# An attention and feed-forward chain on one core: row sums of a head group turned once, inverted on VectorE and brought back as broadcast rows through DRAM

## The chip, the cores and the metric

One NeuronCore of one Trainium2 chip runs the whole program. The metric is the device time of one execution in microseconds (us), the median of several runs. Engines are named as in the profile: PE (TensorE's matmuls) and PEld (its weight loads), DVE (VectorE), ACT (ScalarE), POOL (GpSimd), SP (SyncE, which here issues nearly all DMAs, in the order of its queue).

## The reference, cut to what matters

Eight batches of 512 rows of 512 numbers pass through two transformer layers: a cross attention of 16 heads of 64, then a self attention of 16 heads of 32, a cross attention of 16 heads of 32 and a feed-forward part of width 2048, each with a residual and a layer norm.

```python
# layer 0: heads of 64, added scores and a key mask
attn = softmax(where(mask == 0, NEG_INF, (q @ w_q)h * scale @ (k @ w_k)h.T + add_attn))
out  = (attn @ (v @ w_v)h) @ w_o + residual ; layer norm
# layer 1: heads of 32
x = _ln(x + _mha(x, x, ..., mask)); x = _ln(x + _mha(x, memory, ..., None))
x = _ln(x + relu(x @ w1 + b1) @ w2 + b2)
# the softmax's division by the sum of its row is what the change is about
```

## The kernel before, in words

The program is written engine by engine, with semaphores. It has four attention stages, `L0a` and `L0b` (8 heads of 64 each: the two halves of layer 0), `SA` and `CA` (16 heads of 32), and then the feed-forward part. Every stage runs over the eight batches. Work of one batch is laid out in slots: slot s holds the score product (`SCORE`) of tile s, a tile being 128 query rows of one head against 512 keys. There are 4 tiles to a head, so 32 slots to a batch in `L0a` and `L0b` and 64 in `SA` and `CA`. A head group is what fills 128 columns of output: two heads (8 tiles) or four (16 tiles), so there are 4 groups to a batch and 128 in the run. The tables `WIDE` (L0a, L0b), `SECOND` (SA) and `THIRD` (CA) give, for each step, its slot after the last head's first tile of a group; every engine runs its share of the steps in the order of these slots, and `STEPS` breaks ties.

A tile's way: PE makes the scores in one of two PSUM banks `psS` (L1547, L1548 or L1551). DVE takes them out with the row's smallest value (`MAX`, L2084 or L2088) into one of the tiles `PR`. ACT makes the exponential in place and leaves the row's sum in a column of `SM` (`EXP`, L1883). Then either PE turns the tile with four 128x128 transposes into one of three PSUM banks `psT` (`TURN`, L1572) and DVE or ACT copies it out (`P_LO`, L2180; `P_HI`, L1902), or the tile is split into half words (`SPLIT`, L2188, L1892 or L2464) and turned by two DMAs through `split_rows` (`BOUNCE`, L1349; `FETCH`, L1357), both on SP's queue. The value product of a group (`PV`, L1603) goes to the one PSUM bank `psV`, with rows that are not yet divided by their sums.

The division, as it was: DVE inverts the group's sums `SM` (128x8 or 128x16 numbers) into `RS` (`RECIP`, L2109). POOL spreads them to 128x512 in `RB`, which is the fourth tile of `PR` (`SPREAD`, L2475). PE turns that with four transposes into a bank of `psT` (`R_TURN`, L1580). ACT copies `psV` to `OG`, once the last use of `OG` (`GROUP_LO`, L2120) is over (`GATHER`, L1867). DVE multiplies the two (`SCALE`, L2114). ACT and DVE then make the two parts of `OT`, the input of the output product (`GROUP_HI`, L1876; `GROUP_LO`, L2120). In `SA` and `CA` these two steps of a batch's first group stand late, at slots 22.5 to 25, since `OT` is still read by the output product of the batch before. Because `RB` is a tile of `PR`, the tiles rotate over three buffers and tiles 7 and 15 share the fourth with it.

The order in which an engine works is fixed, so an instruction that waits holds back everything behind it. The score product of a tile waits until the bank of the tile two before it has been taken out by DVE:

```python
pe.wait_ge(s_evac, tal["s"].done(n - 2))
```

## Time and profile before

| | |
|---|---|
| median of 3 runs | 3869.85 us (3869.42 to 3872.04) |
| span of the profiled execution | 3867.5 us |
| the runs' median over that span | 2.35 us more (launch and end) |
| PE busy | 3727.1 us, 96% |
| DVE, ACT, POOL busy | 70%, 58%, 50% |
| DMA: mean of the 16 engines | q1 52.8%, q10 3.3% |

The profiled execution's own time is its span, 3867.5 us, with 2.35 us around it to the median of the runs. A row of a timeline begins with the start of the instruction from the span's start and its length, both in us; xN at its end says that N like it follow each other. Idle time before an instruction stands in brackets, with what ended it. Matmuls are pipelined: the next one starts before the one before has ended, so what one costs is read from start to start.

### The profile page before, as it was taken

Reading aid. Unit: us, or ns where it says so; the run is one execution under the profiler, and the core shown is the slowest. Engines: PE = TensorE matmul, PEld = TensorE weight load, DVE = VectorE, ACT = ScalarE, POOL = GpSimd, SP = SyncE. Lnnn points to the kernel's source line nnn. Section 1 sums busy time; section 2 is a strip of 40 time slices with the busy share of each in tenths; the row PEclk is TensorE's granted clock in tenths of the full one; section 3 lists DMA queues with packets and bytes.
Section 4 is the critical chain, followed back from the end, with each engine's and each line's share of the span. In section 5 each row is a group of like instructions: output and inputs, shape, how many; then the busy total and the mean of one; then the engine's idle time right before and its main releaser. Section 6 shows DMA issues by size and latency. Waiting matters only on the chain.

```text
span 3867.5 us, 63405 instructions
## 1 busy us (share of the span) xinstructions
PE 3727.1 (96%) x20588; PEld 2777.3 (72%) x20588; DVE 2714.5 (70%) x5753; ACT 2233.2 (58%) x4852; POOL 1950.0 (50%) x1981
## 2 busy tenths in 40 slices
PE   9999999999999998999999999999999989999999
PEld 6767777677777766777676766666766768888887
DVE  6666666577777768888888887888888864444434
ACT  6555555555555546888888777788777762111111
POOL 5544445444544445777777656677676642111101
PEclk9999999999999999999999999999999999999999
DMA  6677777545544566666666547666666773122200
GB/s 191 196 207 208 198 193 203 143 136 140 136 132 133 136 185 172 172 172 169 170 169 169 149 145 191 175 169 161 168 169 166 180 218 98 61 71 68 67 26 33
DMA packets 867943, 584.64 MB, mean 151 GB/s; under 512 B 641824, under 2 KB 690976, under 8 KB 866592
## 3 DMA queue, kind: packets, MB, share of 16 engines
q1 hardware_dynamic: 853648, 538.63, 52.8%
q10 hardware_dynamic: 13968, 41.95, 3.3%
q8 instruction: 169, 2.77, 0.3%
q14 instruction: 158, 1.29, 0.1%
HBM read 189.29 MB, written 237.50 MB: 110 GB/s over the span
## 4 chain that ended last, share of the span: by engine, by line
PE 44%; POOL 5%; ACT 5%; issue 5%; DVE 5%; DMA 1%; SPq 0%; DVEq 0%; ACTq 0%; POOLq 0%
PE psV L1603 6%; PE psT L1572 5%; POOL QS L2440 4%; PE psS L1551 4%; PE psJ L1496 3%; PE psJ L1498 3%; PE psJ L1497 3%; PE psS L1498 3%; PE psS L1496 3%; PE psS L1497 3%; PE psT L1496 2%; PE psT L1498 2%; PE psT L1497 2%; ACT PR L1883 2%; PE psT L1580 1%
## 5 line engine op out<-in xcount | busy, mean ns | idle before, releaser
L2440 POOL TENSOR_SCALAR QS<-QK 32x1024 fp32r<-32x1024 f32 (+2 forms) x1152 | 1241.5, 1078 | 858.3 <-DVE QK L2102 435.5
L1883 ACT ACTIVATE PR<-PR,MN 128x512 f32<-128x512 f32 x1536 | 1100.9, 718 | 515.9 <-DVE MN L2084 419.7
L2084 DVE CUSTOM_DVE_ANT_0 PR<-psS,RAW 128x512 f32<-128x512 f32 x1024 | 694.4, 682 | 437.6 <-PE psS L1548 344.2
L1572 PE MATMUL psT<-ID,PR 128*128 128x128 f32 x3912 | 597.0, 275 | 59.4 <-ACT PR L1883 58.4
L1572 PEld LDWEIGHTS psT<-ID,PR 128*128 128x128 f32 x3912 | 470.2, 141 | 211.2 <-ACT PR L1883 110.4
L1603 PE MATMUL psV<-plain 128*32 128x512 f32 (+1 forms) x3072 | 509.0, 609 | 18.2 <-DMA plain<-split_rows 12.5
L1551 PE MATMUL psS<-QS 128*128 128x512 f32 x1024 | 450.6, 442 | 23.2 <-DVE PR L2088 9.2
L2088 DVE TENSOR_SCALAR_CACHE_REDUCE PR<-psS 128x512 f32<-128x512 f32 x512 | 345.4, 682 | 101.1 <-PE psS L1551 98.3
L1922 ACT ACTIVATE PR<-psS,COLS 128x512 f32<-128x512 f32 x128 | 88.3, 690 | 562.6 <-PE psS L1498 562.6
L2180 DVE COPY plain<-psT 128x512 f32<-128x512 f32 x530 | 361.6, 682 | 1.0 <-PE psT L1572 0.8
L1902 ACT ACTIVATE plain<-psT 128x512 f32<-128x512 f32 x448 | 263.9, 589 | 129.6 <-PE psT L1572 127.3
L2154 DVE CAST QK<-PR 128x512 fp32r<-128x512 f32 x128 | 62.3, 487 | 352.1 <-ACT PR L1922 317.2
L1883 ACT ACTIVATION_READ_ACCUMULATOR PR<-PR,MN 128x1 f32 x1536 | 290.7, 189 | 0.0
L1603 PEld LDWEIGHTS psV<-plain 128*32 128x32 f32 (+1 forms) x3072 | 113.9, 118 | 229.2 <-issue 206.7
L1551 PEld LDWEIGHTS psS<-QS 128*128 128x128 f32 x1024 | 194.4, 190 | 106.5 <-DVE PR L2088 31.3
L1496 PE MATMUL psJ<-xT,W 128*128 128x512 f32 x640 | 264.1, 413 | 3.4 <-POOL xT L2388 2.0
L2357 POOL TENSOR_TENSOR Y<-Y,ROWS 128x512 f32<-128x512 f32 x96 | 135.1, 1425 | 237.8 <-DMA Y<-x 226.9
L1498 PE MATMUL psJ<-xT,W 128*128 128x512 f32 x640 | 251.3, 393 | 0.0
L1497 PE MATMUL psJ<-xT,W 128*128 128x512 f32 x640 | 251.1, 392 | 0.0
L2102 DVE SCALAR_TENSOR_TENSOR QK<-psJ,COLS,QK 128x512 fp32r<-128x512 f32 x256 | 190.6, 745 | 80.6 <-ACT QK L1859 80.4
L1547 PE MATMUL psS<-QS 128*128 128x512 f32 x512 | 233.2, 455 | 10.7 <-DVE MN L2084 6.1
L1859 ACT ACTIVATE QK<-psJ,COLS 128x512 fp32r<-128x512 f32 x256 | 173.9, 679 | 112.2 <-PE psJ L1498 86.6
(162 smaller groups left out, 8433.2 us busy)
## 6 DMA issues: line engine op xcount, KB each, us to landing
split_rows<-plain SPq DMA_DIRECT2D x366, 256.0 KB, 2.6
split_rows<-RAW SPq DMA_DIRECT2D x192, 256.0 KB, 2.5
x<-Y SPq DMA_DIRECT2D x96, 256.0 KB, 2.4
RAW<-x SPq DMA_DIRECT2D x96, 256.0 KB, 3.4
Y<-x SPq DMA_DIRECT2D x96, 256.0 KB, 3.2
kept_c<-R SPq DMA_DIRECT2D x32, 512.0 KB, 4.4
kept<-ROWS SPq DMA_DIRECT2D x32, 512.0 KB, 3.8
R<-kept_c ACTq DMA_DIRECT2D x8, 2048.0 KB, 9.0
```

The costliest lines, as they stand in the source:

```text
L1496: nc.tensor.matmul(dst, a[0], b[0], start=first, stop=False)
L1497: nc.tensor.matmul(dst, a[0], b[1], start=False, stop=False)
L1498: return nc.tensor.matmul(dst, a[1], b[0], start=False, stop=last)
L1551: mm = nc.tensor.matmul(psS[:, n % 2], q[:, tile], kk, start=True, stop=True)
L1572: mm = nc.tensor.transpose(dst[:, kt * P:(kt + 1) * P], prob(st, k)[:, kt * P:(kt + 1) * P], ID[:, :])
L1603: mm = nc.tensor.matmul(psV[j * dk:(j + 1) * dk], value(st, h, kt), probs(ring(st, b, h), kt), start=kt == 0, stop=kt == NT - 1)
L1883: nc.scalar.activation(prob(st, k), prob(st, k), ACT.Exp, bias=MN[:, k % 8:k % 8 + 1], scale=-1.0, accum_out=row_sums(st, SM, g)[:, qt, j: ...
L1902: nc.scalar.activation(probs_of(ring(st, b, h), qt), full, ACT.Copy).then_inc(p_copied, 1)
L2084: nc.vector.tensor_tensor_reduce(out=prob(st, k), in0=psS[:, n % 2], in1=FB[:, k % NT], scale=-st.scale, scalar=BIG, op0=ALU.add, op1=ALU. ...
L2088: nc.vector.tensor_scalar(prob(st, k), psS[:, n % 2], -st.scale, None, ALU.mult, ALU.min, accum_out=MN[:, k % 8:k % 8 + 1]).then_inc(s_eva ...
L2180: nc.vector.tensor_copy(probs_of(ring(st, b, h), qt), full).then_inc(t_evac, 1)
L2440: nc.gpsimd.tensor_scalar(to, pair, 1.0, 1.0, ALU.mult, ALU.mult).then_inc(stacked, 1)
```

## The change

The sums of a group are no longer spread before they are turned. `SM` is now two tiles of 128x128, zero outside the sums; PE turns one of them with one transpose as soon as the group's last exponential is done. The first 8 or 16 rows of the result hold one row of 128 queries for each head and query tile. DVE inverts these rows straight out of PSUM into `RT` (8x128 or 16x128). SP stores `RT` to `r_rows` in DRAM (`R_STORE`) and loads each head's row of 512 numbers back as 64 or 32 equal rows of `OG` (`R_LOAD`: two loads a group in L0a and L0b, four in SA and CA). DVE multiplies `psV` by `OG` into `OG`. The steps `SPREAD`, `PASS` and `GATHER` are gone, `R_TURN` and `RECIP` stand earlier or later in the tables, and `PR` rotates over all its four buffers. The output that ACT's `SQUARE` writes only for its sum goes to free parts of other tiles in place of `SPARE`. The rest of the diff keeps the orders and waits right.

```diff
 WIDE = {
...
-    "GATHER": 10.75,
-    "RECIP": 8,
-    "SPREAD": 9.5,
-    "R_TURN": 10.5,
-    "PASS": 11,
-    "SCALE": 12,
+    "R_TURN": 5,
+    "RECIP": 5.5,
+    "R_STORE": 6.5,
+    "R_LOAD": 8,
+    "SCALE": 11.5,
...
 SECOND = {
...
-    "GATHER": 10.5,
-    "RECIP": 5,
-    "SPREAD": 6,
-    "R_TURN": 10.25,
-    "PASS": 11,
-    "SCALE": 12,
+    "R_TURN": 5.5,
+    "RECIP": 6,
+    "R_STORE": 6.5,
+    "R_LOAD": 9.5,
+    "SCALE": 11.5,
...
         PR = sb("PR", [P, 4, S])
-        RB = PR[:, 3]
...
-        SM = sb("SM", [P, 2, 4 * NT])
-        RS = sb("RS", [P, 2, 4 * NT])
+        SM = sb("SM", [P, 2, P])
+        RT = sb("RT", [P, P])
...
         def prob(st, k):
 
-            if k in beside(st):
-                return PR[:, 3]
-            return PR[:, (k - sum(1 for b in beside(st) if b < k)) % 3]
+            return PR[:, k % 4]
...
+            def r_store(tile):
+
+                n = group_at[tile]
+                sp.wait_ge(*evacuated[tile[0], tile[1], ("R", tile[2])])
+                if n > 2:
+                    sp.wait_ge(r_full, loaded_of[n - 2])
+                rows = stage_of[tile[0]].per_group * NT
+                sp.dma_start(r_rows[n % 2].rearrange("j (t q) -> (j t) q", t=NT)[0:rows], RT[0:rows, :]).then_inc(r_stored, 16)
+
+            def r_load(tile):
+
+                n, st = group_at[tile], stage_of[tile[0]]
+                sp.wait_ge(r_stored, 16 * n)
+                sp.wait_ge(o_lo, n)
+                for j in range(st.per_group):
+                    sp.dma_start(OG[j * st.dk:(j + 1) * st.dk, :], r_rows[n % 2, j:j + 1, :].to_broadcast([st.dk, S])).then_inc(r_full, 16)
...
             def turn_reciprocals(st, g, b):
-                i = tal["spread"].next()
-                pe.wait_ge(r_spread, tal["spread"].done(i))
+                pe.wait_ge(exp_done, exp_at[st.name, b, st.per_group * NT * (g + 1) - 1])
                 dst = turn_place(st, b, ("R", g))
-                for tt in range(NT):
-                    mm = nc.tensor.transpose(dst[:, tt * P:(tt + 1) * P], RB[:, tt * P:(tt + 1) * P], ID[:, :])
-                mm.then_inc(t_full, 1)
+                nc.tensor.transpose(dst[:, 0:P], SM[:, g % 2], ID[:, :]).then_inc(t_full, 1)
...
-            def gather(st, g):
...
-                nc.scalar.activation(OG[:, :], psV[:, :], ACT.Copy).then_inc(pv_evac, 1)
...
-            def row_reciprocals(st, g):
-                i = tal["exp"].marked(NT * ((g + 1) * st.per_group - 1) + NT - 1)
-                dve.wait_ge(exp_done, tal["exp"].done(i))
-                nc.vector.reciprocal(row_sums(st, RS, g), row_sums(st, SM, g)).then_inc(recip_done, 1)
+            def row_reciprocals(st, g, b):
+                dve.wait_ge(t_full, turned_at[st.name, b, ("R", g)])
+                dve.wait_ge(r_stored, 16 * (group_at[st.name, b, g] - 1))
+                rows = st.per_group * NT
+                nc.vector.reciprocal(RT[0:rows, :], turned((st.name, b, ("R", g)))[0:rows, 0:P]).then_inc(t_evac, 1)
 
             def scale_group(st, g, b):
-                dve.wait_ge(t_full, turned_at[st.name, b, ("R", g)])
-                dve.wait_ge(pv_evac, tal["pv_own"].done(tal["pv_own"].n - 1))
-                nc.vector.tensor_tensor(OG[:, :], turned((st.name, b, ("R", g))), OG[:, :], ALU.mult).then_inc(t_evac, 1)
+                n = tal["pv"].next()
+                dve.wait_ge(r_full, parts_loaded[st.name, b, g])
+                dve.wait_ge(pv_full, tal["pv"].done(n))
+                nc.vector.tensor_tensor(OG[:, :], psV[:, :], OG[:, :], ALU.mult).then_inc(pv_evac, 1)
...
-            def spread(st, g):
```

How the steps stand now is shown at the second head group of batch 2 of `SA`, the one in which the rows of the timelines below lie. On DVE, around the reciprocal, before (the first row with 512 is `MAX`, `ISA MN` reads out its result, `COPY plain<-PR` is `SPLIT`, `COPY plain<-psT` is `P_LO`):

```order
L2109 RECIPROCAL RS<-SM 128x16 [waits exp_done]
L2084 ISA PR,MN<-psS,RAW 128x512 [waits s_full,t_full]
L2084 ISA MN 128x1
L2188 COPY plain<-PR 128x1024 [waits bounced0,exp_done]
L2084 ISA PR,MN<-psS,RAW 128x512 [waits s_full,t_full]
L2084 ISA MN 128x1
L2180 COPY plain<-psT 128x4x128 [waits t_full]
```

The same place now:

```order
L2088 ISA PR,MN<-psS,RAW 128x512 [waits s_full,t_full]
L2088 ISA MN 128x1
L2114 RECIPROCAL RT<-psT 16x128 [waits r_stored,t_full]
L2194 COPY plain<-PR 128x1024 [waits bounced0,exp_done]
L2088 ISA PR,MN<-psS,RAW 128x512 [waits s_full,t_full]
L2088 ISA MN 128x1
```

The reciprocal has moved one `MAX` later, stands right ahead of a `SPLIT`, and waits for PE's turn in place of ACT's exponential.

On PE, around that turn, now (`psS<-QS` is `SCORE`, `psJ<-W,OT` the output product of the batch before):

```order
L1585 MATMUL psT<-ID,PR 128x128 x4
L1509 MATMUL psJ<-W,OT 128x512
L1510 MATMUL psJ<-W,OT 128x512
L1511 MATMUL psJ<-W,OT 128x512
L1591 MATMUL psT<-ID,SM 128x128
L1564 MATMUL psS<-QS 128x512
L1509 MATMUL psJ<-W,OT 128x512
L1510 MATMUL psJ<-W,OT 128x512
```

It has taken its place ahead of a `SCORE`. Before, the four turns stood behind the value product of the group:

```order
L1572 MATMUL psT<-ID,PR 128x128 x4
L1551 MATMUL psS<-QS 128x512
L1603 MATMUL psV<-plain 32x512 x8
L1580 MATMUL psT<-ID,PR 128x128 x4
L1551 MATMUL psS<-QS 128x512
L1496 MATMUL psJ<-xT,W 128x512
```

The one turn of `SM` (`psT<-ID,SM`) stands about five slots earlier than the four turns of `RB` (the second `psT<-ID,PR`) stood, ahead of the value product.

On SP, between the loads of the sums and what follows them, now (`t_evac` is given by the reciprocal, `o_lo` by `GROUP_LO`, `r_stored` by the landing of the store):

```order
L1359 DMA r_rows<-RT 16x128 [waits r_full,t_evac]
L1341 DMA split_rows<-plain 128x1024 [waits fetched0,p_split]
L1254 DMA RAW<-x 128x512 [waits x_hi]
L1341 DMA split_rows<-plain 128x1024 [waits fetched1,p_split_act]
L1367 DMA OG<-r_rows 32x512 [waits o_lo,r_stored]
L1367 DMA OG<-r_rows 32x512 x3
L1349 DMA_TRANSPOSE plain<-split_rows 128x4x256 [waits pv_full,bounced0]
L1254 DMA RAW<-x 128x512 [waits x_hi]
L1300 DMA kept<-QS 128x2x512 [waits tile_lo]
```

One store and four loads have come in; the first load waits for the store and for the `GROUP_LO` of the group before, and the `FETCH` behind them waits with it.

## Rows read from the trace of the kernel before

**Rows 1.** The page, part 1: busy us (share of the span) xinstructions.
```profile
PE 3727.1 (96%) x20588; PEld 2777.3 (72%) x20588; DVE 2714.5 (70%) x5753; ACT 2233.2 (58%) x4852; POOL 1950.0 (50%) x1981
```

**Rows 2.** Windows L0a, L0b, SA, CA: us, busy of PE, PEld, DVE, ACT, POOL.
```profile
55.00:750.00 695.00, 676.87 (x3601) 492.83 (x3600) 433.37 (x911) 386.93 (x821) 337.95 (x321) 1.00 0.70 191
750.00:1460.00 710.00, 697.39 (x3691) 504.90 (x3690) 509.80 (x1055) 375.88 (x803) 312.64 (x341) 1.00 0.53 143
1460.00:2310.00 850.00, 806.55 (x5053) 590.06 (x5052) 731.40 (x1640) 661.74 (x1498) 585.92 (x582) 1.00 0.64 166
2310.00:3160.00 850.00, 798.83 (x4916) 574.39 (x4915) 710.99 (x1614) 660.06 (x1486) 562.18 (x563) 0.99 0.69 178
```

**Rows 3.** Groups by line: busy us, mean ns | idle before.
```profile
L2120 DVE SCALAR_TENSOR_TENSOR OT<-OG,COLS,OT 128x512 fp32r<-128x512 f32 x128 | 129.3, 1010 | 8.7 <-ACT OT L1876 7.6
...
L2475 POOL TENSOR_SCALAR PR<-RS 128x512 f32<-128x512 f32 x128 | 82.7, 646 | 146.2 <-DVE RS L2109 134.9 <-issue 9.5 <-POOL QS L2440 0.2
...
L1580 PE MATMUL psT<-ID,PR 128*128 128x128 f32 x512 | 81.9, 282 | 0.7 <-DVE plain L2180 0.7
L1867 ACT ACTIVATE OG<-psV 128x512 f32<-128x512 f32 x128 | 76.6, 599 | 180.3 <-PE psV L1603 175.0 <-DVE OT L2120 5.1
```

**Rows 4.** Timeline of PE, SA, batch 2, at two turns of four.
```profile
1709.51 0.60 PE L1572 MATMUL psT<-ID,PR 128*128 128x128 f32 x4
1709.86 0.48 PE L1496 MATMUL psJ<-W,OT 128*128 128x512 f32 x1
...
1724.18 0.66 PE L1580 MATMUL psT<-ID,PR 128*128 128x128 f32 x4
1724.59 0.47 PE L1551 MATMUL psS<-QS 128*128 128x512 f32 x1
```

**Rows 5.** Groups of DVE by line and shape: busy us, mean ns.
```profile
L2180 DVE COPY plain<-psT 128x512 f32<-128x512 f32 x530 | 361.6, 682 | 1.0 <-PE psT L1572 0.8
...
L2109 DVE RECIPROCAL RS<-SM 128x16 f32<-128x16 f32 x64 | 15.6, 243 | 0.5 <-ACT PR L1883 0.5
L2109 DVE RECIPROCAL RS<-SM 128x8 f32<-128x8 f32 x64 | 12.3, 192 | 0.0
```

**Rows 6.** Timeline of DVE, SA, batch 2, where the reciprocal will stand.
```profile
1715.98 0.68 DVE L2084 CUSTOM_DVE_ANT_0 PR<-psS,RAW 128x512 f32<-128x512 f32 x1
1716.59 1.06 DVE L2188 COPY plain<-PR 128x1024 uint16<-128x1024 uint16 x1
...
1717.57 0.67 DVE L2084 CUSTOM_DVE_ANT_0 PR<-psS,RAW 128x512 f32<-128x512 f32 x1
```

**Rows 7.** Timeline of PE, same place: three score products.
```profile
1716.78 0.40 PE L1551 MATMUL psS<-QS 128*128 128x512 f32 x1
...
1717.71 0.39 PE L1551 MATMUL psS<-QS 128*128 128x512 f32 x1
...
1718.39 0.47 PE L1551 MATMUL psS<-QS 128*128 128x512 f32 x1
```

**Rows 8.** Timeline of DVE, same group, around its GROUP_LO and SCALE.
```profile
1723.25 1.69 DVE L2120 SCALAR_TENSOR_TENSOR OT<-OG,COLS,OT 128x512 fp32r<-128x512 f32 x1
...
1726.68 0.68 DVE L2114 TENSOR_TENSOR OG<-psT,OG 128x512 f32<-128x512 f32 x1
```

**Rows 9.** Timeline of ACT, same stretch: the copy of psV.
```profile
1725.03 0.60 ACT L1867 ACTIVATE OG<-psV 128x512 f32<-128x512 f32 x1 [0.37 <-DVE OT L2120]
```

**Rows 10.** Timeline of SP, where the four row loads will stand.
```profile
1718.06 0.42 SPq L1263 DMA_DIRECT2D RAW<-x  x1
...
1721.21 1.28 SPq L1357 DMA_TRANSPOSE plain<-split_rows  x1
```

**Rows 11.** DMA issues: KB each, median us from issue to landing.
```profile
ROWS<-in_key_mask SPq DMA_DIRECT2D x15, 256.0 KB, 4.0
...
COLS<-in_cols SPq DMA_DIRECT2D x1, 20.0 KB, 2.6
```

**Rows 12.** Waits of PE over the run: us in total, times, longest.
```profile
PE psT L1572 <- ACT PR L1883: 58.4, 83, 1.8
```

More of the change, by code:

```diff
@@ L283 @@
     "PV": (8.5, 8.5, 9, 10),
-    "GATHER": 11,
-    "RECIP": 5,
-    "SPREAD": 6,
-    "R_TURN": 10,
-    "PASS": 11,
-    "SCALE": 12,
+    "R_TURN": 5.5,
+    "RECIP": 6,
+    "R_STORE": 6.5,
+    "R_LOAD": 9.5,
+    "SCALE": 11.5,
     "GROUP_HI": (22.5, 13.5, 12, 13.5),
@@ L413, in timetable @@
                 add(NT * h + table["PV"][kt], "PV", (g, kt))
-            add(NT * h + table["GATHER"], "GATHER", g)
-        if last:
-            for step in ("RECIP", "SPREAD", "R_TURN", "PASS", "SCALE", "GROUP_HI", "GROUP_LO"):
+            for step in ("R_TURN", "RECIP", "R_STORE", "R_LOAD", "SCALE", "GROUP_HI", "GROUP_LO"):
                 after = table[step]
@@ L871, in build @@
         QK = sb("QK", [P, 4, S], F32R)
+        with nc.sbuf_tensor("wide", [P, 2, 3, S], F32) as LOOSE:
+            pass
         QS = sb("QS", [P, 2, 3, S], F32R)
         PR = sb("PR", [P, 4, S])
-        RB = PR[:, 3]
         OT = sb("OT", [P, 2, NG, S], F32R)
@@ L1141, in build @@
         sent_at = {tile: n for n, tile in enumerate(orders["SPLIT"])}
+        loaded_of = {n: parts_loaded[tile] for tile, n in group_at.items()}
         split_at, splits = {}, {p_split: 0, p_split_act: 0, p_split_pool: 0}
@@ L1174, in tile_before @@
             last = STAGES[(i - 1) // B]
-            if k in beside(st):
-                return (st.name, b, ("R", 0)) if k == 15 else (last.name, (i - 1) % B, ("R", NG - 1)) if i else None
-            mine, others = ([n for n in range(s.steps) if n not in beside(s)] for s in (st, last))
-            at = mine.index(k) - 3
-            return (st.name, b, mine[at]) if at >= 0 else (last.name, (i - 1) % B, others[at + len(others)]) if i else None
+            return (st.name, b, k - 4) if k >= 4 else (last.name, (i - 1) % B, k - 4 + last.steps) if i else None
         order = weight_order()
@@ L1388, in run @@
                         {"F_LOAD": f_load, "F_BOUNCE": f_bounce, "F_FETCH": f_fetch}[step](at, k)
+                        continue
+                    if step in ("R_STORE", "R_LOAD"):
+                        b = batch + off if at is None else at
+                        (r_store if step == "R_STORE" else r_load)((st.name, b, k))
                         continue
@@ L1974, in run @@
                     elif step == "SQUARE":
-                        square(k)
+                        square(st, k, batch + off if at is None else at)
                     elif step == "CENTRE" and by_parts(st):
@@ L2014, in _ @@
             nc.vector.memset(COLS[:, NCOL:NCOL + NG], 0.0).then_inc(const_ready, 1)
+            nc.vector.memset(SM[:, :], 0.0).then_inc(const_ready, 1)
             dve.sem_inc(s_evac, 2)
@@ L2229, in run @@
                     elif step == "RECIP":
-                        row_reciprocals(st, k)
+                        row_reciprocals(st, k, batch + off if at is None else at)
                     elif step == "SCALE":
@@ L2507, in run @@
                         stack_piece(st, *k)
-                    elif step == "TURN" and k in beside(st):
-                        beside_turn[0] = turned_at[st.name, batch + off if at is None else at, k]
                     elif step == "SPLIT" and split_by_pool(st, k):
                         split_prob(st, k, batch + off if at is None else at)
-                    elif step == "SPREAD":
-                        spread(st, k)
                     elif step == "RES":
@@ L2517, in run @@
                         else:
-                            if st is None and k == 0:
-                                rows_of("FF")
+                            rows_of("FF" if st is None else st.rows)
                             residual(k)
```

89 lines of the change are left out of this document (38 added, 51 removed), and 4 rows, old and new, of the table SEAM.

## The prediction, made before the changed kernel ran

> **What bounds the kernel now.** I read the page's part 1 first: PE is busy 96% of the span, DVE 70% [rows 1]. Next come the windows of the four attention stages, since a mean over the run hides where another engine limits. In L0a and L0b PE is busy for 676.87 of 695 us and 697.39 of 710, while DVE has work for 62% and 72%. In SA and CA PE is busy for 806.55 and 798.83 of 850, and DVE for 86% and 84% [rows 2]. So the first two stages are PE's alone, and in the last two PE loses 43 and 51 us, with DVE close behind. The waits say how: the largest wait of PE is its turn waiting for an exponential, 58.4 us in 83 places [rows 12], and that exponential waits for DVE's `MAX`. The changed steps occur 128 times, 64 in L0a and L0b and 64 in SA and CA (16 batches of four groups). A thing saved on PE counts in full everywhere that PE is not waiting; a thing added on DVE is free in L0a and L0b, and in SA and CA it counts wherever `MAX` has no slack left.
>
> **PE: three turns fewer.** Four turns in a row last 0.60 us, and what follows starts 0.35 us after the first of them; since one lasts 0.27, their starts are (0.60 - 0.27) / 3 = 0.11 us apart [rows 3, 4]. The mean of 0.64 us busy a group [rows 3] is not what they cost, because they overlap their neighbours: from the first reciprocal turn to the next product it is 0.41 us [rows 4]. Three turns fewer are 0.33 us, times 128 = 42 us. The bounds are 0 (where PE waits for DVE anyway) and 0.41 us a group, 52 us, if the remaining turn hid altogether.
>
> **DVE: the reciprocal is the hidden price.** The scaling stays one 128x512 operation. The reciprocal goes from 8 or 16 numbers a partition to 128. It uses fewer partitions, but a partition's numbers pass one after another. An ordinary copy of 512 numbers lasts 682 ns, at most 1.3 ns a number; the reciprocal lasts 192 ns for 8 and 243 ns for 16 [rows 5], so (243 - 192) / 8 = 6.4 ns a number. For 128 numbers that is 243 + 112 x 6.4 = 0.96 us. The bounds are 682 / 4 = 0.17 us, if it ran like a copy, and 0.243 x 8 = 1.94 us, if the whole of it grew with the numbers. I take 0.96, because the two rows are the same operation. With the 0.2 us of the old one gone, DVE gains about 0.75 us of work a group, 96 us in all. 1.94 and 0.17 stay as the ends of the range.
>
> It also waits. It stands behind the `MAX` that ends at 1716.66, and PE comes to the turn only after the product that stands before the score at 1716.78 [rows 6, 7]. With 0.27 us for the turn, DVE can begin at about 1717.1, not at 1716.6: 0.5 us. So what stood at 1716.59, a `SPLIT`, begins 0.5 + 0.96 - 0.24 = 1.2 us later (0.24 is the old reciprocal, gone from just before), and so does the `MAX` behind it, at 1717.57, which ends at 1718.24. The next but one score, at 1718.39, needs the bank that this `MAX` frees [rows 6, 7]: 0.15 us of slack. PE loses 1.1 us. Behind it DVE has no pause up to the scaling, so the delay stays.
>
> In the three other groups of such a batch other work stands around the same slots. I take nothing for the first, whose reciprocal is soon followed by idle time, and 0.75 and 1.0 us for the third and fourth: a choice between nothing and the whole 1.2. A batch: 1.1 + 0.75 + 1.0 = 2.85 us, times 16 = 46 us. Bounds: 0, if the reciprocal costs 0.17 us and the turn is in time, and about twice that at 1.94 us. In L0a and L0b, where DVE is idle for 38% and 28% of the time [rows 2], I take 0.1 us a group, 6 us.
>
> **SP and the way through DRAM.** The copy of `psV` by ACT waited for the last use of `OG`: in the second group of a batch of SA or CA that is the `GROUP_LO` of the first group, which ends at 1724.94, and the copy starts 0.09 us later [rows 8, 9]. Now SP's loads wait for the same end. SP itself would be there at 1721.2 [rows 10], so `GROUP_LO` is what ends last. A DMA issue of a load takes SP 0.42 us [rows 10], so the last of four is issued 1.3 us after the first. The smallest DMA of the run, 20 KB, lands in 2.6 us, a 256 KB broadcast in 4.0 [rows 11]; one of these loads writes 64 KB. I take 1.3 + 2.5 = 3.8 us and the rows are there at 1728.7. DVE stands at `SCALE` at 1726.68 [rows 8]. It will wait 2.0 us, in the second group of each batch of SA and CA. Both ends of this comparison move together with DVE's delay, so that does not hide it. Bounds: 2.6 us in all (0.8 us of wait) and 1.3 + 4.0 = 5.3 (3.5 us of wait). Behind `SCALE` on DVE stand a `SPLIT` and two `MAX`, for which PE waits. 16 x 2.0 = 32 us. And in this group PE saves nothing, because DVE sets the pace: 16 x 0.33 = 5 us are given back.
>
> The Trainium skill gives a fixed cost of about 2.0 us for a DMA, most of it until the write is confirmed (DMA: Bandwidth & Descriptors, Anatomy of one DMA); it would leave the wait near 1.5 us, an estimate. No small load of rows is in this trace to decide.
>
> In the other groups `GROUP_LO` is long over, and the time for the loads is that from SP's place to `SCALE`, here 1726.68 - 1721.21 = 5.5 us [rows 8, 10]: above the 3.8, so I cost them at nothing. If the loads took 5.3 us they would begin to show, by perhaps 0.5 us in 48 groups, 24 us. In L0a and L0b the tables leave 3.5 slots of 710 / 256 = 2.8 us [rows 2], 9.7 us. The `FETCH` behind the loads comes up to 6 us later; the value product reads its tile some 15 slots on, at 850 / 512 = 1.7 us each, so nothing is late. The store goes out when the reciprocal ends, about 1718.1, and 2.6 us later it has landed, before `GROUP_LO` ends.
>
> **What else goes away.** POOL loses 128 spreads of 646 ns, ACT 128 copies of 599 ns [rows 3]. POOL is idle half of the time [rows 1]. ACT is busy 78% of SA and CA [rows 2], and the copy of `psV` itself came after idle time [rows 9]. Some of DVE's operations stretch (this `GROUP_LO` took 1.69 us, the mean is 1.01 [rows 3, 8]), perhaps beside POOL's, and fewer of these would help. I give 10 us for all this; between 0 and 30. The fourth buffer of `PR` lets `MAX` run one tile further ahead of the turns, but no wait of DVE for a turn is among the large ones: nothing. The memset of `SM` and the new waits at the start of the feed-forward part are under 1 us.
>
> **The sum.** -42 (turns) + 6 (reciprocals, L0a and L0b) + 46 (reciprocals, SA and CA) + 32 (waits for rows) + 5 (saving lost there) - 10 (POOL and ACT) = +37 us on the profiled 3867.5, and with the 2.35 us around it 3907 us. A local loss can shrink, since a late PE gives DVE room at the next place, so I go 2 us lower: 3905, 0.9% slower than the median of 3869.85.
>
> **Rivals.**
> 1. *PE's saving alone.* DVE's added work lies in its idle time (14 to 38% of the stages), and the rows are there when `SCALE` comes. For it: 96% on PE, and DVE never at 90%. Against it: 0.15 us of slack behind the second group's reciprocal, and a chain of 3.8 us for which there are 1.8. It gives 3870 - 42 = 3828, with the relief of ACT and POOL up to 10 less. It decides if the reciprocal lasts under 0.4 us, or if the rows land within 1.8 us of `GROUP_LO`. Chance 0.29.
> 2. *Half and half.* The reciprocal costs what I say, but its delay is mostly taken up by waits that PE has there already (43 and 51 us), and only the wait for the rows shows: -42 + 6 + 32 + 5 = about 3870, no change. Chance 0.17.
> 3. *A third price.* The broadcast loads land slowly, as the 4.0 us row says, and then the other groups of SA and CA wait too: 37 + 16 x 1.5 + 24 = 85 us, 3955. For it: all 32 rows of a load come from the same 2 KB. Chance 0.08.
> 4. *My forecast*, both DVE prices biting: 3880 to 3935. Chance 0.46.
>
> **How the numbers follow.** 0.2% of this time, 7.7 us, is about what a measurement of this kernel can tell from no change. Slower: 0.46 + 0.08 + 0.03 of the second case = 0.57. Same: 0.12 of the second case. Faster: 0.29 + 0.02 = 0.31. The range has to reach to the first rival, down to 3832 (some of that case lies below), and up to 3945. The forecast's own range is 3880 to 3935.
>
> **What would show it.** The reciprocal's row on DVE near 0.96 us, with idle time ended by PE's turn in SA and CA. `SCALE` idle before it about 2 us in one group of four of SA and CA, ended by a DMA, and no such wait in L0a and L0b. PE's idle time in the SA and CA windows up from 43 and 51 us to about 75 to 85 each, and the L0a and L0b windows shorter by some 8 us each. The prediction is wrong at its root if the reciprocal is short, or if the row loads land early.

## The result, and the profile after

The changed kernel takes 3944.89 us (median of 4 runs, 3942.07 to 3949.14) against 3870.94 for the kernel before on the same chip: 1.0187 times as long, interval 1.0173 to 1.0202 (the two medians alone would give 1.0191). That is 74 us more, where 35 had been forecast. The profiled execution has a span of 3940.3 us.

Part 1 of the page of the changed kernel answers to [rows 1], and the windows of its four attention stages and of the feed-forward part to [rows 2]. They are cut at most 2 us before each stage's first `MAX`, the last one at CA's last (each row: from and to, us, then the busy time of each engine with its instructions, the granted clock, the DMA share, GB/s):

```profile
PE 3715.4 (94%) x20204; PEld 2739.5 (70%) x20204; DVE 2763.4 (70%) x5754; ACT 2166.6 (55%) x4724; POOL 1895.6 (48%) x1853
```

```profile
25.00:734.00 709.00, 673.57 (x3542) 486.63 (x3541) 462.04 (x930) 381.79 (x812) 330.55 (x295) 1.00 0.72 203
734.00:1457.00 723.00, 689.67 (x3628) 498.91 (x3627) 527.00 (x1047) 356.88 (x765) 291.24 (x308) 1.00 0.57 151
1457.00:2326.00 869.00, 807.64 (x4928) 579.50 (x4926) 740.14 (x1652) 648.25 (x1472) 579.95 (x550) 0.99 0.67 175
2326.00:3212.00 886.00, 808.85 (x4842) 569.67 (x4843) 725.58 (x1626) 647.38 (x1466) 558.21 (x541) 0.99 0.70 177
3212.00:3940.00 728.00, 715.91 (x3169) 588.38 (x3167) 296.41 (x481) 120.91 (x193) 119.38 (x144) 0.99 0.24 69
```

Measured from `MAX` to `MAX`, the stages of the kernel before last 704, 710, 855, 853 and 720 us and those of the changed kernel 710, 724, 868, 887 and 727, so every one is longer now: by 6, 14, 13, 34 and 7. PE has fewer matmuls and does less in L0a and L0b, and still stands idle for 35 and 33 us there, where it was 19 and 11; in SA and CA it idles 61 and 77 us, where 75 to 85 each had been forecast.

The groups of DVE by line and shape (busy us, mean ns, then idle time before them and what ended it) answer to [rows 5]; the group of PE is that of the new turn:

```profile
L2120 DVE TENSOR_TENSOR OG<-psV,OG 128x512 f32<-128x512 f32 x128 | 87.8, 686 | 63.7 <-DMA OG<-r_rows 63.7
L2114 DVE RECIPROCAL RT<-psT 16x128 f32<-16x128 f32 x64 | 60.4, 944 | 29.0 <-PE psT L1591 29.0
L2114 DVE RECIPROCAL RT<-psT 8x128 f32<-8x128 f32 x64 | 60.2, 941 | 10.9 <-PE psT L1591 10.9
```

```profile
L1591 PE MATMUL psT<-ID,SM 128*128 128x128 f32 x128 | 36.9, 288 | 48.3 <-DVE plain L2186 46.4 <-ACT PR L1886 1.3
```

The reciprocal lasts about what was forecast, 0.94 us. `SCALE` waits for its rows, as forecast, but for more groups: of the 63.7 us, 29.4 are the second groups of SA and CA, 20.5 are CA's third groups and 13.1 are one single wait at CA's last group. And one wait was in no step of the prediction: PE's turn of the sums waits 46.4 us for DVE's `P_LO` (L2186), which takes an earlier tile out of `psT`; these are 48 waits of 1.0 us on average, 2.2 at most, and 43 of the 46.4 us lie in L0a and L0b. The timeline of PE in L0b shows one of the shorter ones, with the instruction behind it that starts as soon as the turn does, and the row of DVE that ends it (start, us, and in brackets the idle time before):

```profile
602.60 0.60 PE L1585 MATMUL psT<-ID,PR 128*128 128x128 f32 x4
603.47 0.30 PE L1591 MATMUL psT<-ID,SM 128*128 128x128 f32 x1 [0.27 <-DVE plain L2186]
603.52 0.48 PE L1509 MATMUL psJ<-xT,W 128*128 128x512 f32 x1
```

```profile
602.64 0.68 DVE L2186 COPY plain<-psT 128x512 f32<-128x512 f32 x1
```

The new turn comes directly behind that of a tile (602.60), and before that one PE had turned tiles at 601.70 and 598.72. There are three banks, so it needs the bank of the turn at 598.72, and DVE's copy frees a bank only at 603.32. The four old turns stood 5.5 slots later in the table.

In SA and CA the second group of a batch waits as forecast. This is DVE in CA, the place that answers to [rows 8]:

```profile
2729.38 1.24 DVE L2126 SCALAR_TENSOR_TENSOR OT<-OG,COLS,OT 128x512 fp32r<-128x512 f32 x1
...
2734.46 0.69 DVE L2120 TENSOR_TENSOR OG<-psV,OG 128x512 f32<-128x512 f32 x1 [2.02 <-DMA OG<-r_rows]
```

In CA the third group waits too, in seven of eight batches, and longer. Timelines of ACT, SP and DVE around one, and then the view of its row loads:

```profile
2860.44 0.33 ACTq L1793 DMA_DIRECT2D R<-kept_c  x1
```

```profile
2862.98 2.67 SPq L1367 DMA_DIRECT2D OG<-r_rows  x4
```

```profile
2872.08 0.69 DVE L2120 TENSOR_TENSOR OG<-psV,OG 128x512 f32<-128x512 f32 x1 [3.62 <-DMA OG<-r_rows]
```

```profile
L1367 SPq DMA_DIRECT2D OG<-r_rows x4: 434/532/1031, 2863.0 to 2865.2; - x4
...
DMA to landing us min/median/max: 5.4/6.5/7.2
```

The loads went out in time and took 6.5 us to land; 2.5 us ahead of them ACT had issued a load of 2 MB. The DMA issues of the run (KB each, median us to landing) have 2.1 us for such a load:

```profile
OG<-r_rows SPq DMA_DIRECT2D x128, 128.0 KB, 3.0
OG<-r_rows SPq DMA_DIRECT2D x256, 64.0 KB, 2.1
R<-kept_c ACTq DMA_DIRECT2D x8, 2048.0 KB, 9.5
```

Most of the 7 us behind CA is one wait of PE, before the value product of the last group; the profile does not say what ended it:

```profile
3227.87 5.90 PE L1613 MATMUL psV<-plain 128*32 128x512 f32 x32 [5.28 <-issue]
```

No wait of PE this long stands there in the other runs, whose feed-forward parts last 719 to 726 us. So of the 74 us some 5 may belong to this place alone.

### The profile page after: what moved, and what is told of

It reads as the page before. It is cut to its first block, busy times and chain, and to the rows that moved or that the text cites. A ratio compares the mean times of both kernels' runs of the same rounds, so it can differ in the third digit from the quotient of the medians.

```text
span 3940.3 us, 63021 instructions
## 1 busy us (share of the span) xinstructions
PE 3715.4 (94%) x20204; PEld 2739.5 (70%) x20204; DVE 2763.4 (70%) x5754; ACT 2166.6 (55%) x4724; POOL 1895.6 (48%) x1853
## 4 chain that ended last, share of the span: by engine, by line
PE 36%; DVE 7%; ACT 6%; issue 6%; DMA 4%; POOL 3%; SPq 1%; DVEq 0%; ACTq 0%; POOLq 0%
PE psV L1613 5%; PE psT L1585 4%; PE psS L1564 3%; PE psS L1509 3%; PE psS L1510 3%; PE psS L1511 3%; POOL QS L2444 3%; PE psJ L1509 2%; PE psJ L1510 2%; PE psJ L1511 2%; PE psT L1509 2%; PE psT L1511 2%; PE psT L1510 2%; ACT PR L1886 2%; DMA OG<-r_rows 2%
## 5 line engine op out<-in xcount | busy, mean ns | idle before, releaser
L2186 DVE COPY plain<-psT 128x512 f32<-128x512 f32 x530 | 360.3, 680 | 0.0
```

Source lines behind the costliest of these rows:

```text
L2186: nc.vector.tensor_copy(probs_of(ring(st, b, h), qt), full).then_inc(t_evac, 1)
```

## The experiments

Each run has its own kernel before beside it, so the times below are compared by their ratios to it; 0.1% is 3.9 us. Where a term is given in us it is the difference of two ratios times 3870, and uncertain by some 8 us. Intervals are about 0.15% either way. Lengths of stages come from each kernel's one profiled execution, between the first `MAX` of two stages, and for CA to the end of its last (704, 710, 855 and 853 us in the kernel before, 710, 724, 868 and 887 in the changed one). The diffs are shortened: entries of a table stand on one line, and helper lines are left out.

**turn_later: 1.0137 (1.0121 to 1.0152), 3921.31 us.**

```diff
-    "R_TURN": 5,   "RECIP": 5.5, "R_STORE": 6.5,
+    "R_TURN": 6,   "RECIP": 6.5, "R_STORE": 7,
```

> The changed kernel with three numbers of the table for L0a and L0b changed: R_TURN 5 becomes 6, RECIP 5.5 becomes 6.5, R_STORE 6.5 becomes 7. Theory A, that PE's turn of the sums stands too early and holds PE until a bank of psT is free (46.4 us of idle time before L1591, 43.3 of it in L0a and L0b): these waits fall under 10 us, PE idles 19 and 10 us again in the two stages, and the run is 25 to 40 us shorter than the changed kernel, 3905 to 3920. Theory B, that this wait only stands where PE would wait a moment later for DVE or ACT anyway: under 10 us shorter. If the rows then come late, DVE waits before SCALE in L0a and L0b, which it does not do now.

```profile
L1591 PE MATMUL psT<-ID,SM 128*128 128x128 f32 x128 | 35.9, 280 | 11.4 <-DVE plain L2186 10.8
```

The waits fell from 46.4 to 10.8 us, and the time by 0.50%, 19 us. L0b went back from 724 to 712 us. L0a did not get shorter (712 after 710): there PE's projections of the output now wait for DVE's sum, 9.0 us in 8 places, instead of 5.1 in 3, and 6.8 us of the stage run at a granted clock of 0.50, where the changed kernel had none. The rest of the profiled gain, 12 us, lies in SA, CA and the part behind, whose code is the same, so this pair alone leaves the price open between 9 and 19 us. A second pair helps: turn_rows is the same edit on rows_apart, and there L0a and L0b are 3 and 17 us shorter, and the time falls by 0.42%, 16 us. Neither theory had it whole; the wait was paid, at about half of its length in the mean. The edit moves DVE's reciprocal with the turn, and what that alone is worth was not tried.

**short_recip: 1.0114 (1.0097 to 1.0132), 3914.82 us.** It leaves out the inversion of 112 of 128 row sums.

```diff
-nc.vector.reciprocal(RT[0:rows, :], turned(...)[0:rows, 0:P])
+nc.vector.reciprocal(RT[0:rows, 0:16], turned(...)[0:rows, 0:16])
```

> The changed kernel with a reciprocal of 16 columns of the turned tile and not 128; the other 112 columns of RT keep a constant, so 112 of 128 row sums of each head are not inverted. All waits, turns, stores and loads stay. The reciprocal should last about 0.25 us and not 0.94, 0.7 us less in 128 groups, 89 us of DVE. Theory A, the forecast's term of 46 us for SA and CA is right: 40 to 60 us shorter than the changed kernel, nearly all of it in SA and CA. Theory B, DVE's added time is mostly covered and the changed kernel loses by its waits (turn before a bank is free, rows late): under 20 us shorter.

```profile
L2115 DVE RECIPROCAL RT<-psT 8x16 f32<-8x16 f32 (+1 forms) x128 | 31.0, 243 | 39.6 <-PE psT L1591 39.6
```

0.70 us less in each of 128 groups, and 28 us less in all: SA 10, CA 14, L0b 2, L0a nothing (7 longer in this execution, where 14 us run at a granted clock of 0.50 and in the changed kernel none). Between the theories: the place was right. The forecast has 46 us for a delay of 1.2 us a group; for 0.7 us that would be 27, and SA and CA gave back 24, so this run does not tell whether the term is too large.

**recip_twice: 1.0348 (1.0326 to 1.0371), 4005.08 us.**

```diff
+nc.vector.reciprocal(RT[32:32 + rows, :], turned(...)[0:rows, 0:P])
 nc.vector.reciprocal(RT[0:rows, :], turned(...)[0:rows, 0:P])
```

> The changed kernel with the reciprocal of the turned sums done twice in a row, the first time into rows of RT that nothing reads: 0.94 us more of DVE in each of 128 groups. Theory A, the price is proportional: 30 us for 0.7 us in the short reciprocal gives 40 us more for 0.94, 3985. Theory B, the slack of SA and CA is used up by the first reciprocal, so that the second counts in full in SA and CA, 64 x 0.94 = 60 us and more. Theory C, PE's waits take most of it up: under 20 us.

0.95 us more a group cost 62 us: L0a 18, L0b 5, SA 30, CA 14. A us of DVE in all groups cost 28 / 0.70 = 40 us below the changed kernel and 62 / 0.95 = 65 above it. Each of the two prices is uncertain by 10 us and more, so it is likely, and not more than that, that the price is not proportional: the first part of an addition finds room, the next finds less.

**rows_apart: 1.0126 (1.011 to 1.0141), 3919.5 us.**

```diff
+def rows_at(st, b, g):   # OG in L0a, L0b and the last group of CA
+    return PLAIN[:, 1, 1] if st.name == "SA" and b < B - 1 else LOOSE[:, 0, 2]
-sp.wait_ge(o_lo, n)
+sp.wait_ge(o_lo, n) if to is OG else sp.wait_ge(pv_evac, n)
+dve.wait_ge(o_lo, group_at[st.name, b, g])
-nc.vector.tensor_tensor(OG[:, :], psV[:, :], OG[:, :], ALU.mult)
+nc.vector.tensor_tensor(OG[:, :], psV[:, :], rows_at(st, b, g)[:, :], ALU.mult)
```

> The changed kernel, but in SA and CA (all groups but the last of CA) the broadcast rows go into a tile of their own, so that SP's loads wait for the group before to be scaled (the SCALE before) and no longer for its GROUP_LO, which comes up to 13 slots later; SCALE reads psV and that tile and writes OG as before, and waits for the last GROUP_LO on its own engine. Theory A, the late rows are what SA and CA lose (63.7 us of idle time of DVE before SCALE, of which about 50 in SA and CA): the waits of the second group fall under 0.3 us each and the run is 25 to 45 us shorter. Theory B, DVE's reciprocals set the loss: the waits go, but under 12 us of time with them, since the same operations then wait for something else. In CA's third group, where the wait was not forecast, it stays if it is SP's queue that brings the loads late, and goes if it was GROUP_LO.

Groups of DVE in this kernel, `SCALE` by the tile that it reads (`OG`: L0a, L0b and CA's last group, `plain`: SA but its last batch, `wide`: that batch and CA):

```profile
L2133 DVE TENSOR_TENSOR OG<-psV,OG 128x512 f32<-128x512 f32 x65 | 44.4, 683 | 7.6 <-DMA OG<-r_rows 7.6
L2133 DVE TENSOR_TENSOR OG<-psV,wide 128x512 f32<-128x512 f32 x35 | 24.0, 686 | 15.8 <-DMA wide<-r_rows 15.8
L2133 DVE TENSOR_TENSOR OG<-psV,plain 128x512 f32<-128x512 f32 x28 | 19.2, 685 | 3.0 <-DMA plain<-r_rows 2.9
```

The waits of the second groups are gone, but for the first of them in SA (2.9 us), and 24 us with them: SA 6, CA 22 and the part behind CA 6, while L0a and L0b, whose code is the same, are 6 and 5 us longer in this execution. That is how far a stage can move by itself. CA's third group still waits: `GROUP_LO` was not its cause. Theory A, just under its lower end.

**take_early: 1.0233 (1.0212 to 1.0255), 3961.46 us.** It is rows_apart with one more edit.

```diff
-    "C_TAKE": -12.5,
+    "C_TAKE": -15.5,
+act.wait_ge(j_full, tal["j"].done(tal["j"].n - 1))
```

> The rows-apart kernel with one more edit: in CA the 2 MB load R<-kept_c of the next batch's context is issued 3 slots earlier (C_TAKE -12.5 becomes -15.5, with a wait of ACT for the last product that reads the old context). In the changed kernel it is issued at 2860.44, just before the row loads of the third group (2862.98 to 2865.2), which then take a median of 6.5 us to land and not 2.1. Theory A, this traffic is what made the rows of CA's third group late: the waits of 15.8 us in CA that rows-apart left go under 4 us and CA is 6 to 14 us shorter than in rows-apart. Theory B, another load or SP's queue holds them: waits and time as in rows-apart, within 5 us.

Groups of PE and of DVE:

```profile
L1625 PE MATMUL psV<-plain 128*32 128x512 f32 (+1 forms) x3072 | 515.2, 618 | 44.0 <-DMA plain<-split_rows 38.2 <-DVE plain L2200 3.2 <-DVE xT L2048 0.8
```

```profile
L2134 DVE TENSOR_TENSOR OG<-psV,wide 128x512 f32<-128x512 f32 x35 | 24.0, 685 | 0.3 <-DMA wide<-r_rows 0.3
```

Theory A was right on the cause: without the 2 MB beside them the rows are in time (15.8 to 0.3 us). On the time it was wrong by far. The load now stands beside transposing loads (`FETCH`) for which the value product waits, 38.2 us against 9.5 in rows_apart, and CA takes 34 us longer. Of the two places tried, the one beside the rows was the cheaper.

**recip_ahead: 1.0312 (1.0292 to 1.0333), 3990.16 us.**

```diff
+nc.vector.reciprocal(SM[:, g % 2, 0:n], SM[:, g % 2, 0:n]).then_inc(recip_done, 1)
-pe.wait_ge(exp_done, ...)
+pe.wait_ge(recip_done, ...)
-nc.vector.reciprocal(RT[0:rows, :], turned(...)[0:rows, 0:P])
+nc.vector.tensor_copy(RT[0:rows, :], turned(...)[0:rows, 0:P])
```

> The changed kernel with the whole computation kept and the division in another place: DVE inverts the 8 or 16 row sums of a partition in SM ahead of the turn (192 and 243 ns in the kernel before), PE turns the inverted sums, and behind the turn DVE only copies 128 columns out of psT (at the rate of its 512-column copies, 0.68 us, an estimated 0.2 us). DVE has about 0.5 us less in each of 128 groups, and PE's turn waits for DVE and not for the exponential. Theory A, the price goes with the time that DVE spends: the short reciprocal was 30 us shorter for 0.7 us a group, so 15 to 25 us shorter here, most of it in SA and CA. Theory B, PE's turn now waits for DVE: the gain is lost again, within 8 us of the changed kernel.

Group of PE, PE's timeline at one such turn, and the windows around it:

```profile
L1592 PE MATMUL psT<-ID,SM 128*128 128x128 f32 x128 | 41.9, 327 | 124.8 <-DVE SM L2114 124.7
```

```profile
651.27 0.48 PE L1592 MATMUL psT<-ID,SM 128*128 128x128 f32 x1 [2.97 <-DVE SM L2114]
651.40 0.78 PE L1561 MATMUL psS<-QS 128*128 128x512 f32 x1
```

```profile
647.00:650.50 3.50, 1.30 (x10) 0.92 (x8) 3.50 (x8) 3.30 (x8) 3.23 (x3) 1.00 0.63 135
651.00:654.30 3.30, 3.03 (x11) 2.74 (x12) 2.05 (x7) 1.31 (x3) 1.24 (x1) 0.50 0.87 257
```

In SA and CA it was as theory A had it: 6 and 11 us shorter. In L0a and L0b it was worse than theory B: PE runs ahead of DVE, so standing in the same slot behind it makes it wait in 47 of 64 groups, 2.1 us on average (47.3 and 50.4 us in all, where the changed kernel waits 1.0 us in about as many groups for the bank), and the two stages are 34 and 32 us longer. PE's idle time explains 45 of these 66; the other 21 are busy time, for the same matmuls. After this wait of 2.97 us the granted clock is 0.50 (1.2 GHz), and a score matmul takes 0.78 us where others take 0.39 to 0.50. In the changed kernel the granted clock is 1.00 throughout L0a and L0b; here it falls 12 times and 48 us of the two stages run at 0.50. Half of that, 24 us, is an estimate of what it costs, and about the 21. So some of these waits are paid twice.

**all_four: 1.0434 (1.0393 to 1.0476), 4037.97 us.** The edits of turn_later, rows_apart, take_early and recip_ahead together.

> The changed kernel with the four edits together: the turn of the sums one slot later in L0a and L0b, the rows in a tile of their own in SA and CA, the 2 MB load three slots earlier, the sums inverted before the turn. Nothing is left out of the computation. Theory A, the four prices stand apart and add up: 24 + 25 + 20 + 10 = 79 us less than the changed kernel, 3866, no more than the kernel before. Theory B, they overlap in SA and CA, where the same operations of DVE wait: 40 to 60 us less, 3885 to 3905.

Both theories fell, as the two costs just told are in it: PE waits 88.5 us for the inversion in L0a and L0b, and 50.5 us for `FETCH` in CA.

**turn_rows: 1.0084 (1.0067 to 1.01), 3903.31 us.** turn_later and rows_apart together.

> The changed kernel with two of the edits that shortened it alone, the later turn in L0a and L0b (24 us) and the rows in a tile of their own in SA and CA (25 us). They act in different stages, so they should add up: 3945 - 49 = 3896, with L0b near 712 us and SA and CA near 861 and 864. A rival is that the later turn pushes DVE's reciprocal into another wait that one of the stages shows only now: 3905 to 3915.

0.0187 - 0.0084 = 1.03%, 40 us; the two alone gave 19 and 24. They add up.

**act_copy: 1.0039 (1.0025 to 1.0053), 3886.33 us.** `INVERT` is a step of DVE and inverts `SM` as in recip_ahead; the first table is that of L0a and L0b, the second that of SA and CA.

```diff
-    "R_TURN": 5, "RECIP": 5.5, "R_STORE": 6.5, "R_LOAD": 8,
+    "INVERT": 5, "R_TURN": 7, "RECIP": 7.5, "R_STORE": 8,   "R_LOAD": 9,
-    "R_TURN": 5.5, "RECIP": 6, "R_STORE": 6.5,
+    "INVERT": 5, "R_TURN": 6.5, "RECIP": 7, "R_STORE": 7.5,
-nc.vector.reciprocal(RT[0:rows, :], turned(...)[0:rows, 0:P])
+nc.scalar.activation(RT[0:rows, :], turned(...)[0:rows, 0:P], ACT.Copy)
```

> The changed kernel with the whole computation kept, and the division back on 8 or 16 columns: DVE inverts SM in a step of its own (0.19 and 0.24 us, as in the kernel before), PE turns the result 1.5 to 2 slots later, ACT copies 128 columns out of psT, and the store stands a slot behind. DVE's long reciprocal is gone and no engine has got it. Theory A, that what the inverting ahead of the turn lost in L0a and L0b was PE standing right behind DVE in the same slot, and that DVE's time has a price in SA and CA alone: PE's waits before the turn fall under 10 us in all, L0a and L0b are at or under their 704 and 710 us of the kernel before, SA and CA near 857 and 873 as with the short reciprocal, 3890 to 3900 in all. Theory B, any chain of exponential, DVE, PE and another engine for this turn holds PE up somewhere: over 20 us of such waits, 3920 and more.

PE waits 0.5 us in all before the turn. L0a 699 us, L0b 711, SA 854, CA 865. Theory A, and somewhat better than it said: 0.98% under turn_later, 38 us, for what was left of the bank's waits and all of the long reciprocal (L0a 13, L0b 2, SA 11, CA 18). The two are not separated, nor what ACT's copy in the reciprocal's place is worth.

**act_apart: 0.9984 (0.9974 to 0.9995), 3863.57 us.** act_copy with the edit of rows_apart.

> The kernel with the copy on ACT and the rows in a tile of their own in SA and CA: every cost found so far but the 2 MB load beside CA's third group is taken out, and the three fewer turns of PE stay. Theory A, that the loss of the changed kernel is these costs and nothing else: with the waits for rows gone as well, 20 to 25 us under the kernel with the copy on ACT, so 3865 to 3875, and less where the clock dips fewer times. Theory B, that the way through DRAM costs something by its traffic that none of these edits takes out: over 3885.

Windows of L0a, L0b, SA and CA:

```profile
26.00:730.00 704.00, 677.46 (x3548) 489.19 (x3547) 441.09 (x931) 382.82 (x844) 328.69 (x294) 1.00 0.73 205
730.00:1441.00 711.00, 691.79 (x3627) 499.84 (x3625) 505.34 (x1051) 360.62 (x801) 295.51 (x309) 1.00 0.57 154
1441.00:2289.00 848.00, 796.66 (x4919) 579.95 (x4920) 732.27 (x1648) 654.01 (x1502) 561.20 (x549) 0.99 0.68 179
2289.00:3141.00 852.00, 796.38 (x4847) 567.68 (x4846) 711.91 (x1628) 652.00 (x1499) 543.86 (x540) 0.99 0.72 185
```

Theory A by the time: 21 us under act_copy. Without the turn in its early place, the long reciprocal and the late rows of the second groups, the kernel is 79 us shorter, more than the 72 that it had lost. It is the best found that computes everything, and it stands only just under the kernel before, though three turns fewer should have given more (one_turn, below). So something is still paid, and `SCALE` waits 40 us here in all: 19.2 in CA's third groups, 10.2 in L0a and L0b, 7.1 at CA's last group and 3.6 at SA's first second group.

**scale_later: 0.9996 (0.9987 to 1.0005), 3870.92 us.** act_apart with one move in CA.

```diff
-    "SCALE": 11.5,                      "GROUP_HI": (22.5, 13.5, 12, 13.5), "GROUP_LO": (25, 13.5, 13.5, 13.5),
+    "SCALE": (11.5, 11.5, 13.5, 11.5),  "GROUP_HI": (22.5, 13.5, 14, 13.5), "GROUP_LO": (25, 13.5, 15.5, 13.5),
```

> The kernel of the last run (copy on ACT, rows in a tile of their own) with the third group of CA scaled two slots later (SCALE 11.5 becomes 13.5 there, GROUP_HI 12 becomes 14, GROUP_LO 13.5 becomes 15.5), and nothing moved in the DMA queues. There DVE still waits 19.2 us in 8 places, 2.4 us each, for rows that land beside the 2 MB load; two slots are 3.3 us. Theory A, that these waits are paid in full: they go, the 2 MB load stays where it is, CA falls from 852 to about 838 and the run from 3864 to about 3850. Theory B, that MAX and the turns behind them had room by now: the waits go and the time falls by under 6 us.

```profile
L2146 DVE TENSOR_TENSOR OG<-psV,wide 128x512 f32<-128x512 f32 x35 | 23.9, 684 | 0.1
```

DVE's 19.2 us of waiting are gone and no time with them (if anything 5 us more, the intervals overlap). Theory B. The same kind of wait was worth 24 us in the second group, and in the third nothing came back. That the wait is free there is not quite shown: this edit does not bring the rows earlier but moves `SCALE` and what hangs on it later, which may have a price of its own.

**one_turn: 0.9924 (0.9909 to 0.9939), 3840.42 us.** The kernel before; it leaves out three of the four turns of a group.

```diff
-for tt in range(NT):
+for tt in range(1):
```

> The kernel before, with only the first of the four 128x128 turns of the reciprocals in each group; the three others are left out, so that SCALE multiplies three quarters of the columns by what the bank held. Nothing else is changed. Theory A, the forecast's first term: 42 us shorter than the kernel before, 3828 (bounds 0 and 52). Theory B, the turns go while PE would wait anyway in SA and CA: about half, 15 to 25 us.

29 us shorter, not 42: L0a 9, L0b 6, SA 9, CA 5, where 10.6 each were forecast. Between the theories: the number is nearer to theory B, whose upper end is 25, but SA gained as much as L0a, which theory B had excluded.

**no_way: 0.9915 (0.99, 0.993), 3836.43 us.** act_apart; it leaves out the store and all row loads, so nothing is divided by the row sums.

```diff
-(r_store if step == "R_STORE" else r_load)((st.name, b, k))
-nc.vector.tensor_tensor(OG[:, :], psV[:, :], rows_at(st, b, g)[:, :], ALU.mult)
+nc.vector.tensor_scalar(OG[:, :], psV[:, :], 0.01, None, ALU.mult)
```

> The kernel with the copy on ACT and the rows apart, with the store to DRAM and all loads of rows left out: SCALE multiplies psV by the constant 0.01, so nothing is divided by the row sums; the inversion, the turn and the copy stay. It asks what the way through DRAM still costs once its waits are mostly out of the way (DVE idles 33 us before SCALE there). That kernel runs at 3864 and the kernel before with one turn at 3840: 24 us are not explained. Theory A, SP's 512 issues and loads and the waits that are left cost them: 3838 to 3846. Theory B, the way through DRAM is free now and the rest lies with the turn and the copy: within 6 us of 3864.

Windows of L0a, L0b, SA and CA:

```profile
26.00:721.00 695.00, 672.81 (x3546) 487.12 (x3545) 440.36 (x931) 382.02 (x843) 329.43 (x294) 1.00 0.70 195
721.00:1424.00 703.00, 689.49 (x3627) 498.60 (x3626) 504.80 (x1050) 359.83 (x800) 295.03 (x308) 1.00 0.54 143
1424.00:2268.00 844.00, 795.36 (x4930) 580.28 (x4929) 730.08 (x1650) 654.78 (x1503) 564.92 (x550) 1.00 0.66 170
2268.00:3112.00 844.00, 793.60 (x4846) 566.67 (x4845) 717.70 (x1630) 652.59 (x1500) 544.51 (x540) 0.99 0.70 176
```

0.69% under act_apart, 27 us, 5 to 9 in every attention stage, a little under theory A's range. So the way through DRAM costs time in every stage, after the second groups' waits have been cleared away. `SCALE` waits 2.5 us here and 40 in act_apart (33 in the expectation, which leaves out the 7.1 of CA's last group).

**no_division: 0.9894 (0.9877 to 0.9911), 3830.33 us.** no_way; it leaves out the inversion, the turn and the copy too.

```diff
-for step in ("INVERT", "R_TURN", "RECIP", "R_STORE", "R_LOAD", "SCALE", ...):
+for step in ("SCALE", ...):
```

> As the last one, with the inversion on DVE, PE's turn of the sums and ACT's copy left out as well; nothing is left of the division but SCALE by a constant. It bounds what any way of dividing can cost beside SCALE. From the rows the one turn is 0.1 to 0.3 us of PE a group, 13 to 35 us for 128; DVE's 0.2 us and ACT's copy lie beside other work. Theory A: 13 to 20 us under the run without the way through DRAM, 3820 to 3830. Theory B, the turn hides in PE's waits and pauses: under 8 us.

0.21%, 8 us, for all three: theory B, at its edge.

## Why the prediction fell short, step by step

**The sign and three of the mechanisms were right.** The reciprocal was to last 0.96 us and lasts 0.94; DVE does wait 1.0 to 3.6 us in the second group of a batch of SA and CA, mostly 1.5 to 2.2 and 29.4 in all, where 32 were forecast; the two together cost more than the turns save. short_recip shows that the reciprocal's time goes with the columns: 16 columns of 8 or 16 partitions out of PSUM take the 243 ns that 16 columns of 128 took [rows 5], so a column is (943 - 243) / 112 = 6.25 ns, and the number of partitions does not matter. The Trainium skill's repeat count of 8 (VectorE: DVE Perf Modes, First, the fixed hardware budget) had made an estimated 1.07 us of it; the row says 0.94.

**"From the first reciprocal turn to the next product it is 0.41 us", three turns fewer, -42.** one_turn: -29. The turns are really gone from PE (idle time aside, L0a's busy time falls from 684.89 to 673.40 us), but PE then reaches sooner what it waits for: its idle time is 7 us longer over the four stages.

**"A batch: 2.85 us", reciprocals in SA and CA, +46.** Too large: act_copy, which takes the whole delay out, is 28 us shorter than turn_later in the two stages. The guess of 0.75 and 1.0 us for the third and fourth groups, made without a count of their slack, was perhaps the weak place; no run tells the groups apart. The 18 us that the term has too much nearly cancel the next one in the total.

**"L0a and L0b windows shorter by some 8 us each."** The step that failed most: they are 6 and 14 us longer, 36 us in all from the forecast. DVE was idle for a third of the time there, and from that I took the new steps to be almost free. But the turn of the sums needs a bank of `psT`, not only DVE's time, and the prediction put this wait at nothing without giving a reason. The four old turns needed a bank as well, 5.5 slots later, where it was free (0.7 us of waiting in all [rows 3]). In its new place the turn stood close behind two others and held PE until the bank came back. turn_later shows 19 us, with turn_rows 16; act_copy, one slot later still, brings the waits from 10.8 to 0.5 us. The next term adds 16 us in these two stages, and the turns saved 15 there where 21 were forecast.

**"In the other groups ... I cost them at nothing."** no_way shows 27 us for the way through DRAM beyond the second group's waits. It was the largest missing term, and the second step that failed. CA's third group does wait 1.7 to 4.0 us, which was not foreseen, though taking this wait away in scale_later gained nothing. What does cost is only partly known. PE idles 18 us more in act_apart than in no_way over the four stages (704 - 677.46 against 695 - 672.81 and so on: 4, 6, 3, 5). The other 11 us of these executions are busy time, and go with the granted clock: 47 us of the four stages run at 0.50 in act_apart and 24 in no_way, and half of the difference, 12 us, is an estimate of the price. Whether the 14 us that `SCALE` waits in L0a, L0b and SA, SP's 512 issues or the traffic beside the other loads holds PE up, no run here tells apart.

**"In all 3.8 us"**, the chain for the second group, +32 and +5: measured 24 by rows_apart and 21 by act_apart. The Trainium skill's fixed cost of about 2.0 us a DMA (DMA: Bandwidth & Descriptors, Anatomy of one DMA), which the page gives for DMAs that GpSimd issues, fits the loads of 64 KB that SP issues here, median 2.1 us; those beside the 2 MB took 6.5. The same page has a rule for these (DMA: Bandwidth & Descriptors, Queues, rings and completion order): a DMA engine goes round between the queues that have work for it, a whole packet at a time. take_early agrees with it in so far as the lateness went with the 2 MB; how the packets took turns no run here shows.

**"I give 10 us for all this"**, POOL and ACT relieved: no_way, which lacks POOL's spreads and has a copy of 128 columns for one of 512, is 3 us shorter than one_turn, less than the measurement can tell. As far as this comparison goes the term is near nothing; no run takes POOL's or ACT's share alone.

The sum in measured terms: -29 (turns) + 38 (the long reciprocal and the rest of the bank's waits) + 19 (the bank) + 21 (rows of the second group) + 27 (the rest of the way) = 76, where 0.0187 x 3870 = 72 were measured. Four of the five are steps of one chain, from the changed kernel over turn_later, act_copy and act_apart to no_way, so they add up by themselves to what lies between its ends. The test of the sum is the fifth alone: no_way should stand under the kernel before by what the turns save, and it does so by 33 us, where one_turn has 29. Each difference is uncertain by some 8 us.

**The rivals.** The time stands nearest to the third rival's 3955, and that is luck: its loads were to take 4.0 us each, and the loads of 64 KB land in 2.1. The first (3828) had the reciprocal short and the rows in time, and the second (3870) had its delay taken up; neither was so. My own forecast had the two DVE prices biting, as they do, and ended at 3905 because it put two further prices at nothing, the bank and the rest of the way through DRAM.

## What to carry to other kernels

Ask of a moved step which buffers it takes and who holds them at its new place, not only whether its engine has time: an in-order engine that waits for a bank holds back work that is ready. On PE, put a step behind another engine's by 1.5 to 2 slots, not in the same one; the same inversion made PE wait 98 us in L0a and L0b there and not at all two slots later. And an idle time in front of an instruction is no price: waits of some 2 us for the same kind of rows gave back 24 us in the second groups, where the rows were brought earlier, and nothing in CA's third, where `SCALE` was moved later. Only an edit that takes them away can tell.

## What the hardware showed that was not expected

A reciprocal costs by columns alone: 944 ns for 16x128 and 941 for 8x128, and 243 ns for 16 columns, on 8 or 16 partitions out of PSUM as on 128 [rows 5]. Loads of 64 KB that land in 2.1 us (median) took 5.4 to 7.2 beside a 2 MB load on another engine's queue. Right after PE had stood idle 2.97 us the granted clock was 0.50, and 45 us of added idle time in L0a and L0b made 66 us of added time.
